# Transposing h by one crossbar DMA per supertile instead of on TensorE, in a graph-network layer

## The reference

```
h = max(layernorm(x), 0)
hi = h @ W1[:384] + emb[adj] @ W1[384:] + b1        # per pair i, j
hj = h @ W2[:384] + emb[adj] @ W2[384:] + b2
A = softmax over j of where(adj != 0, sum_e(hi * hj), -1e9)
out = x + relu((A @ h) @ gcn_w + gcn_b) @ Wo_w + Wo_b
```

## Time and profile before

| | us |
|---|---|
| median of 3 runs | 427.15 (426.7 to 428.35) |
| the profiled execution, its own time | 427.54 |
| its span | 425.3 |

### The profile page before, as it was taken

One profiled execution on the slowest core, in us unless ns is written; L12 is line 12 of the kernel. 1 busy time (PEld: TensorE's weight loads), 2 busy tenths in 40 slices (PEclk: granted clock), 3 DMA queues, 4 the chain that ended last, 5 costly groups with the idle time before them and its releaser, 6 DMA issues.

```text
span 425.3 us, 10122 instructions
## 1 busy us (share of the span) xinstructions
PE 377.3 (89%) x3260; PEld 237.1 (56%) x3260; DVE 321.3 (76%) x684; ACT 230.0 (54%) x504; POOL 255.9 (60%) x449
## 2 busy tenths in 40 slices
PE   3719486459999999999999999999999999999986
PEld 3314163355757575665656575756565757566654
DVE  1658264386897988888888888888888897968675
ACT  2255524436565647474747475655555564745441
POOL 2413230798858676777768585858586868681811
PEclk9967978869999999999999999999999999999999
DMA  8881050034133343434343434343333331323134
GB/s 254 231 227 44 0 153 0 0 76 141 36 102 101 84 131 74 148 74 148 74 148 74 148 74 148 74 131 78 107 88 109 94 92 41 74 75 104 46 76 150
DMA packets 38756, 42.81 MB, mean 101 GB/s; under 512 B 2210, under 2 KB 38692, under 8 KB 38740
## 3 DMA queue, kind: packets, MB, share of 16 engines
q1 hardware_dynamic: 38032, 41.62, 33.9%
q10 hardware_dynamic: 644, 0.79, 0.6%
q0 software_dynamic: 64, 0.20, 0.2%
HBM read 17.44 MB, written 12.58 MB: 71 GB/s over the span
## 4 chain that ended last, share of the span: by engine, by line
PE 75%; issue 10%; POOL 6%; DVE 5%; DMA 2%; ACT 1%; POOLq 0%; DVEq 0%; SPq 0%
PE bank L974 20%; PE bank L975 19%; PE bank L976 19%; PE bank L1031 5%; PE bank L1020 4%; PE bank L1189 3%; PE bank L1184 3%; DMA x_all<-in_x_dram 2%; POOL root_sq L318 2%; PE bank L1137 1%; POOL root L318 1%; DVE stats L595 1%; POOL adj_all L379 1%; POOL g_parts L354 1%; POOL var_d L318 1%
## 5 line engine op out<-in xcount | busy, mean ns | idle before, releaser
L354 POOL TENSOR_TENSOR g_parts<-g,g_parts 128x512 f16<-128x512 f32 x45 | 52.0, 1158 | 68.4 <-DVE g_parts L706 68.4
L974 PE MATMUL bank<-gw_hi,hT_hi 128*128 128x385 f16 (+2 forms) x204 | 65.8, 327 | 15.6 <-DVE hT_lo L601 8.0
L454 ACT ACTIVATE g<-bank,pair_bias 128x512 f32<-128x512 f32 x48 | 32.7, 686 | 62.5 <-PE bank L976 62.4
L401 POOL TENSOR_TENSOR z_lo<-z,z_hi 128x512 f16<-128x512 f32 x46 | 56.5, 1253 | 15.2 <-DVE z_hi L829 15.2
L975 PE MATMUL bank<-gw_lo,hT_hi 128*128 128x385 f16 (+2 forms) x204 | 65.3, 325 | 0.1
L976 PE MATMUL bank<-gw_hi,hT_lo 128*128 128x385 f16 (+2 forms) x204 | 65.3, 325 | 0.0
L459 ACT ACTIVATE hg_hi<-bank 128x384 f16<-128x384 f32 x64 | 31.2, 491 | 52.0 <-PE bank L976 52.0
L974 PE MATMUL bank<-wo_hi,z_hi 128*128 128x384 f16 x180 | 58.7, 326 | 0.0
L975 PE MATMUL bank<-wo_lo,z_hi 128*128 128x384 f16 x180 | 58.7, 326 | 0.0
L976 PE MATMUL bank<-wo_hi,z_lo 128*128 128x384 f16 x180 | 58.7, 326 | 0.0
L974 PE MATMUL bank<-hT_hi,m_hi 128*128 128x512 f16 x144 | 54.7, 380 | 1.2 <-DVE hT_lo L601 1.2
(11 more groups left out here) (128 smaller groups left out, 814.0 us busy)
## 6 DMA issues: line engine op xcount, KB each, us to landing
x_all<-in_x_dram SPq DMA_DIRECT2D x16, 768.0 KB, 5.4
out_dram<-x_all SPq DMA_DIRECT2D x15, 768.0 KB, 3.9
hg_parts<-hg_lo SPq DMA_DIRECT2D x32, 192.0 KB, 3.4
hg_parts<-hg_hi SPq DMA_DIRECT2D x32, 192.0 KB, 3.9
out_dram<-x_all SPq DMA_DIRECT2D x4, 192.0 KB, 1.9
x_all<-in_L_gnn_W_w_dram SPq DMA_DIRECT2D x1, 576.0 KB, 5.6
x_all<-in_L_gnn_W_w_dram ACTq DMA_DIRECT2D x1, 576.0 KB, 6.1
gcn_raw<-in_L_gnn_gcn_w_dram SPq DMA_DIRECT2D x1, 576.0 KB, 11.1
```

The source lines that it names most:

```text
L354: nc.gpsimd.tensor_tensor(g_parts[:, c, :, 1, :], g_graphs[:, c, :, :], g_parts[:, c, :, 0, :], ALU.subtract).then_inc(g_split, 1)
L401: nc.gpsimd.tensor_tensor(z_lo[:, c, :], z32[:, c, :], z_hi[:, c, :], ALU.subtract).then_inc(z_split, 1)
L454: nc.scalar.activation(g32[:, c, :], bank[G_BANK[c]][:, :], ACT.Identity, bias=pair_bias[:, c:c + 1], scale=PROJ).then_inc(g_copied, 1)
L974: nc.tensor.matmul(dst, lh, rh, start=(c == 0), stop=False)
```

## The change

h is no longer transposed on PE. ACT normalises each tile twice, once to f32 (`h_tok`) and once to f16 (`h_parts`, high half); DVE subtracts the two in one instruction over the whole supertile (`token_low`), which gives the low half; then SP issues one transposing DMA (`transpose_h`) from `h_parts` [128, 3072] to `hT[half]` [128, 24, 128], 24 blocks of 128x128 in f16. `hT` exists twice, `h_parts` once. PE's loop body now holds two supertiles, so that the buffer is a constant, and SP's loop is written out.

New places in the programs: `token_low(s+1)` stands at the head of DVE's iteration s; `transpose_h(s+2)` stands in SP's pass s between the load and `move_hg(s+1)`, and waits for scores of s; `normalise(s)` waits until the transposing DMA of s-1 has landed; PE's first matmul of G(s) waits until that of s has. PE's waits that guarded the transposes' banks are gone. To make room, several tiles of the prologue (`product`, `q_row`, `w1_dep`, `w2_dep`, `wo_raw`) now lie inside parts of `x_all` that are loaded later.

```diff
+        h_parts = sb("h_parts", [P, KT, 2, D], f16)
+        hT = [sb(f"hT{b}", [P, KT * 2 * DC, P], f16) for b in range(2)]
+        hT_parts = [t[:, :, :].rearrange("p (k n c) t -> p k n c t", k=KT, n=2) for t in hT]
...
+            def transpose_h(s, half):
+                sp.wait_ge(h_split, s + 1)
+                if s >= 2:
+                    sp.wait_ge(s_done, s - 1)
+                sp.dma_start_transpose(hT[half][:, :, :], h_parts[:, :, :, :].rearrange("p k n d -> p (k n d)"))\
+                  .then_inc(hT_landed, 16)
...
             for s in range(2, 4):
                 sp.wait_ge(x_loaded, 16 * s)
                 load_x(s)
+            transpose_h(0, 0)
...
             move_hg(0)
+            transpose_h(1, 1)
+            for s in range(LAST):
+                if s + 4 <= LAST:
+                    sp.wait_ge(x_loaded, 16 * (s + 4))
+                    load_x(s + 4)
+                if s + 2 <= LAST:
+                    transpose_h(s + 2, s % 2)
                 move_hg(s + 1)
                 store_out(s)
...
             def normalise(s):
...
-                    act.wait_ge(t_done, DC * s)
+                    act.wait_ge(h_split, s)
+                    act.wait_ge(hT_landed, 16 * s)
                 for k in range(KT):
-                    nc.scalar.activation(h_tok[:, k, :], x_all[:, s, k, :], ACT.Relu, bias=ln_add[:, k:k + 1],
-                                         scale=ln_mul[:, k:k + 1]).then_inc(h_ready, 1)
-            def transposed_high(s):
-                if not isinstance(s, int) or s >= 1:
-                    act.wait_ge(s_done, s)
-                for c in range(DC):
-                    act.wait_ge(t_done, DC * s + c + 1)
-                    nc.scalar.activation(hT_hi[:, c, :], bank[T_BANK[c]][:, :], ACT.Copy).then_inc(t_high, 1)
+                    for to in (h_tok[:, k, :], h_parts[:, k, 0, :]):
+                        nc.scalar.activation(to, x_all[:, s, k, :], ACT.Relu, bias=ln_add[:, k:k + 1],
+                                             scale=ln_mul[:, k:k + 1]).then_inc(h_ready, 1)
...
-            def transposed_low(s):
-                for c in range(DC):
-                    dve.wait_ge(t_high, DC * s + c + 1)
-                    nc.vector.tensor_tensor(hT_lo[:, c, :], bank[T_BANK[c]][:, :], hT_hi[:, c, :],
-                                            ALU.subtract).then_inc(t_split, 1)
+            def token_low(s):
+                dve.wait_ge(h_ready, 2 * KT * (s + 1))
+                nc.vector.tensor_tensor(h_parts[:, :, 1, :], h_tok[:, :, :], h_parts[:, :, 0, :],
+                                        ALU.subtract).then_inc(h_split, 1)
...
             def iteration(s, prev=True, prev2=True, cur=True, nxt=True, nxt2=True):
+                if nxt and prev2:
+                    token_low(s + 1)
                 for c in range(DC):
...
-                if nxt and prev:
-                    transposed_low(s + 1)
...
-            def transposes(s, prev=True, after_g=False):
...
-                    pe.wait_ge(t_split, DC * s + d + 1)
+                    pe.wait_ge(hT_landed, 16 * (s + 1))
...
-                                  lambda d: (hT_hi[:, d, rows], hT_lo[:, d, rows]),
+                                  lambda d: (hT_parts[half][:, k, 0, d, :], hT_parts[half][:, k, 1, d, :]),
...
-                if nxt:
-                    transposes(s + 1)
...
+            with pe.Fori(1, LAST // 2) as pair:
+                iteration(2 * pair, 0)
+                iteration(2 * pair + 1, 1)
```

More of the change, by code:

```diff
@@ L114, in gnn_layer_program @@
         m_raw = x_all[:, NSUP - 5, 0:DC, :]
+        product, q_row = (x_all[:, NSUP - 4 + n, DC, :] for n in (0, 1))
+        w1_dep, w2_dep = (x_all[0:DE + 1, NSUP - 4 + n, DC, :] for n in (2, 3))
+        wo_raw = x_all[:, NSUP - 10, 0:DC, :]
         stats6 = sb("stats6", [P, KT, 6])
@@ L664, in _ @@
             magnitude(0, m_raw[:, 0, :], AX.X, m_peaks)
+            token_low(0)
             dve.wait_ge(weight_peaks_all, 1)
@@ L1005, in _, with scores_of, g_chunk @@
                       .then_inc(pq_projected, 1)
[L1007 to L1024 removed]
+            def scores_of(s, half):
                 for k in range(KT):
                     for g in range(GT):
[L1028 removed]
+                        cols = slice(g * S, (g + 1) * S)
                         for d in range(DC):
[L1030 removed]
+                            for n in range(2):
                                 last = nc.tensor.matmul(score_bank[:, k, g, :], g_parts[:, d, GT * k + g, :, :],
[L1032 removed]
+                                                        hT_parts[half][:, k, n, d, cols], start=(d == 0 and n == 0),
                                                         stop=(d == DC - 1 and n == 1))
                 last.then_inc(s_done, 1)
[L1036 removed]
+            def g_chunk(c, half, before=None):
                 split_product(bank[G_BANK[c]][:, :],
                               lambda d: (m_hi[:, d, c * P:(c + 1) * P], m_lo[:, d, c * P:(c + 1) * P]),
[L1039 removed]
+                              lambda d: (hT_parts[half][:, :, 0, d, :], hT_parts[half][:, :, 1, d, :]), before).then_inc(g_done, 1)
             pe.wait_ge(m_copied, DC)
[L1043 removed]
             def chunk_ready(s):
@@ L1114, in _ @@
             for k in range(KT):
-                rows = slice(k * P, (k + 1) * P)
                 last = split_product(bank[7][:, k:k + 1],
-                                     lambda d: (hT_hi[:, d, rows], hT_lo[:, d, rows]),
+                                     lambda d: (hT_parts[0][:, k, 0, d, :], hT_parts[0][:, k, 1, d, :]),
                                      lambda d: (gw_hi[:, d, D:D + 1], gw_lo[:, d, D:D + 1]))
@@ L1122, in _, with iteration @@
             pe.wait_ge(dot_done, 2 * DC + 1)
-            scores_of(0)
-            transposes(1, prev=False, after_g=True)
-            def iteration(s, prev2=True, cur=True, nxt=True):
+            scores_of(0, 0)
+            def iteration(s, half, prev2=True, cur=True):
                 def transposed_attention():
@@ L1159, in iteration @@
                             pe.wait_ge(o_added, KT * (s - 2) + c + 1)
-                        g_chunk(c, chunk_ready(s) if c == 0 else None)
+                        g_chunk(c, half, chunk_ready(s) if c == 0 else None)
                     if c == 0 and prev2:
```

74 lines of the change are left out of this document (18 added, 56 removed).

## The result

The changed kernel takes 440.52 us (median of 4 runs, 439.98 to 440.85) against 427.75 us for the kernel before (median of 4 runs): a ratio of 1.0299, with a 95% interval of 1.0273 to 1.0324. It is slower by 3%. Its profiled execution took 439.98 us with a span of 438.0 us, 12.7 us longer than the span before.

The account below looks back on a forecast made before the run. The prediction took a ring through GpSimd's hold on att as the bound, 22.40 us a period. 12 x 0.7 = +8.4, start +3.5, last step -1.3 made +10.6: 438.1 us, range 431 to 446, with rivals 420 to 470.

Parts of the forecast that it names:

- The ring: Loop: closed chain of GpSimd's bias addition, att, attention transposes, Z, z_lo, coefficients; sets the period, grows 0.7 us.
- E: End of GpSimd's bias addition in a period, from which the ring's times are counted; 211.77 before the change.
- What goes: Loop: TensorE's 1.34 us of transposes and both evictions lie off the ring, worth nothing except at supertile 14 to 15.
- The DMA: Loop: the crossbar transpose of 768 KB takes 6 us, bounds 5.4 and 11.7, and is hidden or just not.
- the tolerance: Loop: about 16.5 us allowed by the ring from token_low's end to the transposing DMA's landing.
- Rival (c): Loop: the transpose lands late, each microsecond past 16.5 adding one per period; near 590 us at 23.4 us; chance 0.18.
- The start: First supertiles: late first landing mostly covered, then token_low meets z_lo and doubled normalisations delay; +3.5 us, bounds 0 and 8.
- (a): Loop: TensorE's gain arrives, 14 x 1.34 = 18.8 us come off, 408.4 us; chance 0.13.
- (b): Loop: the bias addition starts behind att, which then costs 0.42 us; period 22.2, 427 us; chance 0.17.

Follow-up runs that it names:

- the one instruction alone: Kernel before, with token_low's subtraction added at the head of VectorE's iteration, result unused: 437.23 us, 1.0222.
- the run with the earlier issue: Changed kernel with first transposing DMA ahead of the loads, four hg evictions before normalising supertile 2, supertile 3's statistics ahead of token_low: 441.08 us, 1.0309.
- the plain transfer: Changed kernel with the transposing DMA replaced by a plain copy of the same 768 KB: 439.97 us, 1.0268.
- four pieces: GpSimd's bias addition of 128x1536 issued as four of 128x384: on the kernel before 426.02 us, 0.9969; on the changed kernel 434.25 us, 1.0153.

## Why the prediction was right

**The ring, +0.7 a period.** Forecast 22.40 to 23.1, measured 23.12 and, with the one instruction alone, 23.13. The steps hold one by one: `token_low` 1.77 forecast, 1.75 measured; Z at E+6.1, measured E+6.29; `z_lo` at E+9.2, measured E+9.18; `att` held as before, 2.93 us, and by more than the 2.60 of the earlier trace rows, since it is issued 0.33 us earlier on that clock, with `hT_lo` gone. The order of arithmetic was right too: 11 periods of 0.70 and one of 0.47 make 8.2 against the 8.4 of the sum.

**What goes is worth nothing in the loop.** The wait at the attention transposes grew from 5.8 to 17.4 us. At the one step where `att` is free, supertile 14 to 15, 1.35 us were gained, forecast 1.3.

**The DMA, hidden.** The size was low: 6 us were taken and 8.1 measured in the median, 5.5 at the least and 9.4 at the most. It stays inside the bounds of 5.4 and 11.7 and far inside the tolerance. Rival (c) fell: 24 blocks of 128x128 take 8.1 us, 0.34 us a block. The 31 us worked out beside it from the Trainium skill (VectorE: DVE Perf Modes, The three transpose paths) took its figure for one transpose 24 times over, and the run shows that they don't follow one another like that.

**The start, +3.5, was the mis-sized term.** It measured +6.9 by the score copy of supertile 2, inside the bounds of 0 to 8. The first landing was covered, as forecast and as the run with the earlier issue shows. The second transpose is issued behind `token_low` of supertile 1 at 59.6 us, and TensorE waits for it to 65.18:

```profile
65.18 0.61 PE L974 MATMUL bank<-hT,m_hi 128*128 128x512 f16 x1 [7.68 <-DMA hT<-h_parts]
```

where these products started at 60.32 before. This was covered too. GpSimd's first bias addition, which the next scores stand behind, waits for none of these products, and in the run with each transpose done twice they started 14 us later still (79.25) while that addition moved by 2.3 (85.03 to 87.33). But the addition was itself late, 85.03 against 82.55, and this the prediction had in no term. Part of it is in the idle time before GpSimd's last reduction, before and after:

```profile
68.67 0.41 POOL L390 PARTITION_ALL_REDUCE peak_all<-peak_part  x1 [6.15 <-issue]
```

```profile
70.58 0.41 POOL L398 PARTITION_ALL_REDUCE peak_all<-peak_part  x1 [7.51 <-issue]
```

The profile names no releaser for it. It is 5.8 to 6.2 us in the traces of the kernel before and its three variants, and 7.4 to 7.7 in eight of the changed kernel and its variants, where a transposing DMA issued at about 60 us is under way when it begins. With the plain transfer it is 6.3, and 6.2 in the run with each transpose done twice, where that DMA is issued only at 68.2. So some 1.4 us go with the crossbar's DMA; how it delays GpSimd, and where the other 1.1 us come from, stays open. The scores of supertile 1 follow GpSimd and start 2.5 us late (91.85 against 89.38).

Behind that come the terms that the prediction did name, but with both at full size: `z_lo` beside `token_low` and the `hg` parts takes 4.90 instead of 3.40 us, so the third normalisation starts 3.9 us late (103.61 against 99.70), and its four more activations put the attention copy 6.4 us late (109.11 against 102.68). TensorE's lower clock there (0.50 from 96 to 100 us, after a wait of 11.7 us for `g_parts`) is not on this path, since its attention transposes were done at 107.7, before ScalarE took the copy. This last part was read from the two timelines; the run that moved `token_low` there shows that it collides with either neighbour, and no run took the terms apart.

**The tail.** 1.05 us were gained behind supertile 15's scores, which no step had. They are not the change's doing as far as is known: in the profiled execution of the kernel before, TensorE's granted clock was 0.77 from 411 to 415 us and 0.85 from 415 to 420, while in the changed kernel it stayed at 1.00, and the same stretch took 19.7, 20.6 and 21.9 us in the traces of three variants of the kernel before, against 20.4 in this one. With 3.4 us too little at the start, this, and 0.2 less in the loop, the sum of +10.6 stands against +12.7 in the span. That it came so near is in part luck, as the tail took off a third of what the start had too little.

**The rivals.** (a), 408 us, needed `att` free of the bias addition; nothing that was removed did that, and with it partly free (four pieces) 0.6 us a period came, not 1.34. (b), the opened lock with a path through normalisation, `token_low`, `g_high` and copies of 22.2 us, is what the four pieces made of it: 22.49, and its waits are the ones named there. It did not open by itself; `z_lo` came within 0.02 us of where it was placed.

## What to carry to other kernels

An engine that is 89% busy need not be the bound: look for an instruction of another engine that takes several times its usual length, since that is where two engines hold each other and where the loop closes. Moving work off the busy engine pays only if what replaces it is in no ring; here 1.75 us of replacement work in the wrong place cost more than the 1.34 us of transposes that it freed. When such an instruction is moved, list which instructions of the other engine it will run beside at the new place: of the other places tried for `token_low`, two in the loop and one in the start brought no gain, and in two of these it was seen to hold up other instructions of GpSimd; the third in the loop was tried only together with other edits.

## What the runs showed of the hardware

- A transposing DMA of 128x3072 half-precision elements holds SyncE's queue for 6.1 us when a store and a load were issued just before and 3.6 us when the queue had been idle; a plain DMA of the same bytes takes 0.5 us. It lands 5.4 us after issue at best, the plain one 3.6.
- Cutting the instruction that holds a lock into pieces moves the holding to the next instructions: with four pieces of about 1 us, `att` went from 2.93 to 0.50 us, and its two followers from 0.29 and 0.42 to 0.98 and 1.10. The first of these reads only one tile from SBUF, so the hold is not confined to instructions with two such inputs.
- The hold works in both directions: beside `token_low`, GpSimd's `g_parts` took up to 1.2 us longer over two of them, and `token_low` 2.72 us instead of 1.75.
- GpSimd's idle time before a reduction in the start was 7.4 to 7.7 us where a transposing DMA was under way when it began, and 5.8 to 6.3 us where none or a plain one was; no run shows why.
